# Kernel with adjacency blocks turned by DMA, selection steps shifted toward pass 1, all neighbour coordinates by lookups, arctangent one slot behind its quotients

## The reference

```python
def _L0_xattn_ref(xyz, points, w_center, w_neighbor):        # xyz = ctx, points = x, both weights = fside
    K = 8; NUM_BLOCKS = 4
    sq = jnp.sum(xyz * xyz, axis=1)
    d2 = sq[:, :, None] + sq[:, None, :] - 2.0 * jnp.einsum('bdn,bdm->bnm', xyz, xyz)
    _, idx = jax.lax.top_k(-d2, K)
    for i in range(NUM_BLOCKS):
        shortcut = points
        p = _lrelu(points)                                    # slope 0.01
        g = _group_point(p, idx_t)                            # the 8 neighbours' columns of p
        c = jnp.einsum('oi,bin->bon', w_center[i], p)
        gn = jnp.einsum('oi,bikn->bokn', w_neighbor[i], g)
        points = (c + gn.sum(axis=2)) / (K + 1.0) + shortcut
    return points

def _L1_xattn_ref(x_loc, x, ...):                             # x_loc = ctx, x = the result above
    idx = _knn(x_loc, 30)                                     # the same distances, 30 nearest
    rel = pts[bidx, idx] - pts[:, :, None, :]                 # first three coordinates are used
    xr, yr, zr = (rel[..., 0], rel[..., 1], rel[..., 2])
    rho = sqrt(x2 + y2 + z2); theta = arctan2(zr, sxy); phi = arctan2(yr, xr)
    feat = concatenate([sph, sph - mean(sph)])                # six features
    h = lrelu(_bn(feat @ W1.T, g1, b1)); h = lrelu(_bn(h @ W2.T, g2, b2)); h = lrelu(_bn(h @ W3.T, g3, b3))
    att = softmax(h[..., 0])                                  # over the 30 neighbours
    return x + einsum('bnkc,bnk->bnc', xk, att)               # xk: the neighbours' columns of x
```

## Time and profile before

| | |
|---|---|
| median of 3 runs | 698.96 us (698.92 to 703.58) |
| the profiled execution | 703.56 us |
| its span, first to last instruction | 701.8 us |
| mean granted TensorE clock | 0.995 of 2.4 GHz |
| busy over the span | TensorE 97%, VectorE 85%, GpSimd 56%, ScalarE 49% |
| selection, from its first step to the last index table | 32.2 to 285.4 us |

### The profile page before, as it was taken

One profiled execution on the slowest core, in us unless ns is written; L12 is line 12 of the kernel. 1 busy time (PEld: TensorE's weight loads), 2 busy tenths in 40 slices (PEclk: granted clock), 3 DMA queues, 4 the chain that ended last, 5 costly groups with the idle time before them and its releaser, 6 DMA issues.

```text
span 701.8 us, 13118 instructions
## 1 busy us (share of the span) xinstructions
PE 679.3 (97%) x5364; PEld 573.4 (82%) x5364; DVE 599.0 (85%) x879; ACT 346.1 (49%) x529; POOL 394.1 (56%) x324
## 2 busy tenths in 40 slices
PE   5999999999999999999999999999999999999998
PEld 4799889878888887788888987987988877778887
DVE  4699999999789899876679998776895999788866
ACT  6456547347525327766694354384473434233210
POOL 2268757664877877310039677558669865610143
PEclk9999999999999999999999999999999999999999
DMA  9630300200000022644532721713627763621125
GB/s 350 192 4 2 120 1 2 90 21 11 1 2 0 2 65 87 221 152 165 164 114 91 116 79 63 118 61 91 105 76 221 126 90 90 182 77 47 46 92 164
DMA packets 39483, 64.89 MB, mean 92 GB/s; under 512 B 16000, under 2 KB 16256, under 8 KB 39424
## 3 DMA queue, kind: packets, MB, share of 16 engines
q1 hardware_dynamic: 30288, 44.61, 18.9%
q0 software_dynamic: 8608, 18.40, 13.7%
q10 hardware_dynamic: 528, 1.05, 0.4%
HBM read 47.92 MB, written 14.82 MB: 89 GB/s over the span
## 4 chain that ended last, share of the span: by engine, by line
PE 60%; DVE 16%; POOL 11%; issue 5%; ACT 4%; DMA 2%; another core or an unknown queue 1%; SPq 0%; POOLq 0%; DVEq 0%; ACTq 0%
PE bank L1669 17%; PE bank L1731 4%; PE bank L1579 4%; PE bank L1693 4%; PE bank L1581 4%; PE bank L1580 4%; PE bank L1694 4%; PE bank L1695 4%; POOL more L660 4%; PE bank L1834 3%; PE bank L1793 3%; PE bank L1836 3%; PE bank L1835 3%; POOL p_second L590 3%; POOL pts_l L601 2%
## 5 line engine op out<-in xcount | busy, mean ns | idle before, releaser
L1669 PE MATMUL bank<-nbr,pts_h 128*128 128x512 f32 (+2 forms) x512 | 192.9, 379 | 3.2 <-POOL pts_l L601 1.6
L1669 PE MATMUL bank<-nbr,pts_l 128*128 128x512 f32 (+2 forms) x512 | 190.1, 374 | 0.0
L590 POOL TENSOR_TENSOR p_second<-p_first,p_second 128x512 f32<-128x512 f32 x58 | 76.4, 1320 | 99.4 <-ACT p_second L868 99.3
L1669 PEld LDWEIGHTS bank<-nbr,pts_h 128*128 128x128 f32 x512 | 96.6, 189 | 20.8 <-POOL pts_l L601 3.4
L1669 PEld LDWEIGHTS bank<-nbr,pts_l 128*128 128x128 f32 x512 | 96.7, 189 | 14.9 <-issue 0.2
L882 ACT CAST pts_h<-bank 128x512 fp32r<-128x512 f32 (+2 forms) x64 | 35.1, 554 | 144.5 <-PE bank L1669 136.0
L1693 PE MATMUL bank<-wT,pts_h 128*128 128x512 f32 x256 | 102.7, 401 | 1.4 <-DVE pts_l L1172 0.7
L1695 PE MATMUL bank<-wT,pts_l 128*128 128x512 f32 x256 | 100.4, 392 | 0.0
L1694 PE MATMUL bank<-wT,pts_h 128*128 128x512 f32 x256 | 100.2, 392 | 0.0
L601 POOL TENSOR_TENSOR pts_l<-p_second,pts_h 128x512 fp32r<-128x512 f32 x58 | 79.1, 1370 | 3.5 <-ACT pts_h L874 2.0
L1579 PE MATMUL bank<-pts_h 128*128 128x512 f32 (+3 forms) x192 | 68.9, 359 | 8.6 <-DVE pts_l L1098 8.1
(11 more groups left out here) (228 smaller groups left out, 1518.5 us busy)
## 6 DMA issues: line engine op xcount, KB each, us to landing
p_rows<-p_second SPq DMA_DIRECT2D x32, 256.0 KB, 2.0
more<-a_rows SPq DMA_DIRECT2D x16, 480.0 KB, 4.7
scratch<-a_rows SPq DMA_DIRECT2D x14, 480.0 KB, 5.0
X<-in_ctx SPq DMA_DIRECT2D x12, 512.0 KB, 6.1
out_dram<-X SPq DMA_DIRECT2D x15, 256.0 KB
more<-in_ctx SPq DMA_DIRECT2D x4, 512.0 KB, 5.7
X<-in_x SPq DMA_DIRECT2D x2, 1024.0 KB, 5.5
x_rows<-X SPq DMA_DIRECT2D x8, 256.0 KB
```

The costliest lines, as they stand in the source:

```text
L590: pool.tensor_tensor(p, a, b, ALU.subtract).then_inc(s_p32, 1)
L1669: mm = pe.matmul(bank[u % 3][:, 0:w], p[:, m, t * P:(t + 1) * P], nbr[b][:, m, hf * HALF:hf * HALF + w], start=(m == 0 and part_ == 0), st ...
```

## The change

**Turns by DMA.** `adj_turn(T)` leaves TensorE. SyncE issues a transposing DMA of the 128x1024 bf16 matrix, from `adj` to `landing(T)`: for tiles 0 to 6 the columns of tile 7 in `nbr0`, which are not yet written, for 7 to 15 a part of `scratch`. Even and odd tiles have a semaphore each. `nbr_out` reads `landing(T)` instead of a PSUM bank, and `adjacency(T + 2)` waits for the landing of T. In SyncE's queue the turns stand among the loads of X: T 0 and 1 ahead of the first two, 2 to 5 behind them, 6 to 9 behind the third, 10 to 15 behind the fourth. `nbr_out` of tile 7 waits for that of tile 6. `ADJ_AT` moves three of the four pairs one slot later.

**Selection.** The extra steps of slots 0 and 1 go from 4 and 1 to 2 and 1; slot 15 gets one more, slot 16 four more. Steps end at slot 41 instead of 43, so `G0` is 42 instead of 44. The index tables move to slots 28, 31, 34 and 42 from 30, 33, 36 and 44.

**Lookups for all tiles.** The 30 indirect DMAs, the table in DRAM with its three loads, and the copy from `near_rows` are gone. 32 lookups instead of 30 begin at slot 43 instead of 45. `M0` is 60 instead of 61.

**Arctangent.** ScalarE issues it one slot behind item 10's slot (at 76, where `NET` has an empty entry now), and item 11 and all later ones keep their slots. `T0` is 109 in both.

The diff, cut to its core:

```diff
+        def landing(T):
+            if T < NT - 1:
+                c0 = (NT - 1) * P + T % 2 * P // 2
+                return nbr0_land[:].bitcast(BF16)[:, :, 2 * c0:2 * c0 + P]
+            o = (SC + 1) * N + T % 2 * HALF
+            return scratch[:, o:o + HALF].bitcast(BF16).rearrange("p (m n) -> p m n", m=NT)
...
-            n = STEPS_AT[g % 16] + {0: 4, 1: 1}.get(g, 0)
+            n = STEPS_AT[g % 16] + {0: 2, 1: 1, 15: 1, 16: 4}.get(g, 0)
...
-        ADJ_AT = {3: (8, 9), 6: (10, 11), 9: (12, 13), 14: (14, 15)}
+        ADJ_AT = {4: (8, 9), 7: (10, 11), 10: (12, 13), 14: (14, 15)}
...
-        ROWS_AT = {30: 0, 33: 1, 36: 2, 44: 3}
+        ROWS_AT = {28: 0, 31: 1, 34: 2, 42: 3}
...
-        M0 = G0 + LOOKUPS // 2 + 2
-
-        GATHER_AT = {16: 2, 17: 2, 18: 2, 19: 2, 20: 2, 21: 2, 22: 2, 23: 2, 32: 3, 33: 3, 34: 3, 35: 3, 36: 1, 37: 1}
+        M0 = G0 + TILES + 2
...
-               ((8, 1),), ((9, 0),), ((9, 1),), ((9, 2),), (10,), (11,), (12,), (13,), (14,), (15,), (16,), ((21, 0),),
+               ((8, 1),), ((9, 0),), ((9, 1),), ((9, 2),), (10,), (), (11,), (12,), (13,), (14,), (15,), (16,), ((21, 0),),
...
-        T0 = M0 + len(NET) + GT
+        T0 = 16 * (ITS - 2) + 13
...
+            def adj_turn(T):
+                sp.wait_ge(s_diag, T + 1)
+                if T == NT - 1:
+                    sp.wait_ge(s_sqmm, 2 * NH)
+                if T >= 2:
+                    sp.wait_ge(s_nbr, T - 1)
+                sp.dma_start_transpose(landing(T), adj[:, T % 2, :]).then_inc(s_adjT[T % 2], 16)
+
+            adj_turn(0)
+            adj_turn(1)
             for i, (t0, t1) in enumerate(((0, 4), (4, 8))):
 
                 sp.wait_ge(s_pl1, KT + 4 + 2 * i)
                 sp.dma_start(X[:, 0, t0:t1], x[0].rearrange("(t p) c -> p t c", p=P)[:, t0:t1]).then_inc(s_x[i], 16)
             for i, (t0, t1) in enumerate(((0, 6), (6, 8))):
 
+                for T in (range(6, 10) if i else range(2, 6)):
+                    adj_turn(T)
                 sp.wait_ge(s_p1, AHEAD)
                 sp.wait_ge(s_v, TILES - 2 if i else NT - 1)
                 sp.dma_start(X[:, 1, t0:t1], x[1].rearrange("(t p) c -> p t c", p=P)[:, t0:t1]) \
                     .then_inc(s_x[2 + i], 16)
-            sp.wait_ge(s_adjT, TILES)
+            for T in range(NT + 2, TILES):
+                adj_turn(T)
+            sp.wait_ge(s_nbr, TILES)
...
-                    done = sum(GATHER_AT[q] for q in GATHER_AT if q < g)
-                    for i in range(done, done + GATHER_AT.get(g, 0)):
-                        if i == 0:
-                            pool.wait_ge(s_tabd, 16 * 3)
-                            pool.wait_ge(s_sel, GT)
-                        pool.indirect_dma_start(
-                            out=near_rows[:, i // K1, i % K1, :], out_offset=None, in_=tab_d,
-                            in_offset=bass.IndirectOffsetOnAxis(ap=idx[:, i // K1, i % K1:i % K1 + 1], axis=0)) \
-                            .then_inc(s_rows, 16)
...
             def nbr_out(T):
-                act.wait_ge(s_adjT, T + 1)
+                act.wait_ge(s_adjT[T % 2], 16 * (T // 2 + 1))
+                if T == NT - 1:
+                    act.wait_ge(s_nbr, T)
                 if T == NT:
                     act.wait_ge(s_sel, NT)
                 act.copy(nbr[T // NT][:, :, (T % NT) * P:(T % NT + 1) * P],
-                         bank[6 + T % 2][:].bitcast(BF16).rearrange("p (m n) -> p m n", m=NT)) \
-                    .then_inc(s_nbr, 1)
+                         landing(T)).then_inc(s_nbr, 1)
...
+                if 10 in NET_AT.get(g - 1, ()):
+                    act.wait_ge(s_mlp, MLP["atan"])
+                    act.activation(pair(6), tmp, ACT.Arctan).then_inc(s_act, 1)
                 for m in NET_AT.get(g, ()):
                     if m == 4:
                         act.wait_ge(s_mlp, MLP["sqrt"])
                         act.activation(slots(6, 2), slots(4, 2), ACT.Sqrt).then_inc(s_act, 1)
-                    if m == 10:
-                        act.wait_ge(s_mlp, MLP["atan"])
-                        act.activation(pair(6), tmp, ACT.Arctan).then_inc(s_act, 1)
...
-                    dve.wait_ge(s_rows, 16 * GT * K1)
-                    link(dve.tensor_copy(near[:, :, 0:GT, :], near_rows[:].rearrange("p t k j -> p j t k")))
...
-            def adj_turn(T):
-                pe.wait_ge(s_diag, T + 1)
-                if T >= 2:
-                    pe.wait_ge(s_nbr, T - 1)
-                for m in range(NT):
-                    mm = pe.transpose(bank[6 + T % 2][:].bitcast(BF16)[:, m * P:(m + 1) * P],
-                                      adj[:, T % 2, m * P:(m + 1) * P], ident_b[:])
-                mm.then_inc(s_adjT, 1)
```

More of the change, by code:

```diff
@@ L77, in build @@
         pts_l = sb("pts_l", [P, KT, N], F32R)
+        with nc.sbuf_tensor("nbr0_land", [P, NT, N], F32) as nbr0_land:
+            pass
         nbr0 = sb("nbr0", [P, NT, N], F32R)
@@ L109, in build @@
         prm = sb("prm", [P, 77], F32)
-        near_rows = sb("near_rows", [P, GATHERED_TILES, K1, 3], F32)
         w_eff = sb("w_eff", [P, 6, 3], F32)
@@ L117, in build @@
         p_d = [nc.dram_tensor(f"p_rows{i}", [N, C], F32, kind="Internal").ap() for i in range(B)]
-        tab_d = nc.dram_tensor("table", [N, 3], F32, kind="Internal").ap()
         x_d = nc.dram_tensor("x_rows", [N, C], F32, kind="Internal").ap()
@@ L269, in build @@
         s_diag = sem("adj_diagonal_ready")
-        s_adjT = sem("adj_transposed")
+        s_adjT = [sem(f"adj_transposed{i}") for i in range(2)]
         s_nbr = sem("nbr_ready")
@@ L428, in _ @@
                                  allow_slow_non_contiguous=True).then_inc(s_prm, 16)
-            for j in range(3):
-                sp.dma_start(tab_d[:, j].unsqueeze(1), ctx[0, 2 - j, :].unsqueeze(1),
-                             allow_slow_non_contiguous=True).then_inc(s_tabd, 16)
+            def adj_turn(T):
[7 more added lines that the diff above has]
+            adj_turn(1)
             for i, (t0, t1) in enumerate(((0, 4), (4, 8))):
@@ L463, in _ @@
             for c in range(CHUNKS):
-                for t in range(2 * CH) if c else range(2 * GT, 2 * CH):
-                    u = 2 * CH * c + t - 2 * GT
+                for t in range(2 * CH):
+                    u = 2 * CH * c + t
                     if u == 0:
@@ L1647, in _ @@
             gram(15)
-            adj_turn(6)
             norms(1)
@@ L1727, in lookup @@
                 pe.wait_ge(s_ar, CHUNKS)
-                b = (GT + u // 2) // NT
+                b = u // (2 * NT)
                 for k in range(KH):
@@ L1742, in side @@
             def side(g):
-                if g == 1:
-                    adj_turn(NT - 1)
-                for T in ADJ_AT.get(g - 1, ()):
-                    adj_turn(T)
                 if g in TURN_AT:
```

29 lines of the change are left out of this document (9 added, 20 removed).

## The result

The changed kernel takes 695.39 us (median of 20 executions, 693.38 to 697.79) against 699.7 us (median of 20, 698.56 to 703.58). The ratio is 0.9932, 95% interval 0.9917 to 0.9947: 4.7 us less, 3.7 to 5.8. The forecast was 2.4 us less: the time lies in its range, but the gain is about twice the forecast one. The profiled executions lie further apart, 703.56 and 694.02 us, because that of before was one of its slowest and that of after one of its fastest.

A forecast was written before the change was run, and what follows sets the result against it. VectorE was taken to bound the kernel up to the gate (first lookup), TensorE behind it. Terms -9.3 + 7.8 - 0.9 = -2.4 us on the median 698.96 gave 696.6 us, with 691 to 703 for 8 in 10.

The forecast's parts named there:

- the gate: VectorE's last index table and TensorE's first lookup behind it (286.19 us before); forecast to come 9.3 us earlier, near 277.
- VectorE's idle time before the gate: First selection step to last index table: 8.0 of VectorE's 9.3 us of waits would be used.
- TensorE's wait for `q_low` that I had near slot 19: TensorE's 1.5 us wait at slot 3 shrinks and one of about its size appears at slot 19.
- What fills it: Before the gate: turns credited 1.0 us (adjacency wait); moved selection steps fill 5.4 at slot 16, 0.3 and 1.3 elsewhere.
- The index tables: Last index table moves from slot 44 to 42, putting two `x_update` behind the gate: 1.3 us.
- Behind the gate: TensorE gets two more weight units (5.4 us) and two more lookups (2.4 us), giving back 7.8 us.
- GpSimd's 30 indirect DMAs go too ...: 0: Slots 0 to 44: removal gains 0, as only 0.8 us of VectorE's waiting was for GpSimd, before the first of them.
- The stall at slot 79: TensorE's 0.7 us wait at 427.43, 0.9 with restart; a slot of lead around the arctangent covers it, gaining 0.9 us.
- DMA transposes: Turns by DMA take 2.3 us each, hidden between GpSimd's diagonal and ScalarE's `nbr_out`; cost 0 us.
- Rival B: DMA transposes much slower than copies, delaying tiles 2, 3 and pass 0; at 6 us each +10.8, 707.4 us; chance 0.12.
- Rival A: TensorE decides before the gate too: -6.9 for turns, its waits also count; -8.0, 691.0 us; chance 0.13.
- Rival C: Slot 16 steps delay `q_low` more than they fill, or first lookups run late; half of 5.4 lost, 699.3 us; chance 0.13.

The follow-up runs named there:

- turn: Kernel before with only the sixteen turns moved from TensorE to transposing DMAs; 697.46 us, ratio 0.9959.
- sel: Kernel before with only the new slots of selection, adjacencies and index tables, turns still on TensorE; 700.33 us, ratio 1.0008.
- turn_look: Changed kernel with the old slots of selection, adjacencies and index tables, without the arctangent's move (lookups from slot 45, network from 62); 697.07 us, ratio 0.9975.
- turn_sel: Kernel before with the transposing DMAs and the new selection, adjacency and index table slots; lookups and arctangent as before; 698.98 us, ratio 0.9995.
- no_atan: Changed kernel with the Arctan in item 10's slot, no empty entry in `NET`, network from slot 61; 695.11 us, ratio 0.9928.
- slow_turn: Changed kernel with each transposing DMA issued, waited for and issued again; 717.62 us, ratio 1.0281.
- pe_turns: Changed kernel with the turns back on TensorE; 697.14 us, ratio 0.9979.

## Why the prediction was right, and where it was not

The forecast (696.6 us, no change over 1%) holds, and its frame too: sum up to the gate, then what TensorE has left. The size doesn't: 2.4 us is below the measured interval of 3.7 to 5.8. The first lookup came 11.6 us earlier, not 9.3; the other two terms fit. Point by point:

- **VectorE's idle time before the gate: right.** 8.0 us were to be filled, 7.7 were (9.3 to 1.6). TensorE's wait for `q_low` that I had near slot 19 is not there: the 1.5 us stayed at slot 3 (143.21), and 1.3 for GpSimd came up at slot 16.
- **What fills it: wrong.** "TensorE is not the one that decides" before the gate was false at slot 16. The 5.4 us wait there was for TensorE through ScalarE, so the turns counted there: in turn alone VectorE's `q_low` of slot 16 comes 3.8 us earlier (194.77 to 191.00). I had put 1.0 us on the turns and the rest on the shift; turn gives 3.8 us at slot 32 by itself, sel 1.0. The two compete for one wait. That the idle time filled came out right is luck in part: it is bounded by the wait, whatever fills it.
- **The index tables: missed.** VectorE's gate came 12.8 us earlier, not 9.3. Its groups for them, before and after:

```profile
L1189 DVE TENSOR_SCALAR scratch<-idx 128x128 uint32<-128x128 uint32 x4 | 2.5, 632 | 0.0
L1192 DVE CAST scratch<-scratch 128x128 bf16<-128x128 uint32 x4 | 2.5, 617 | 0.1
L1190 DVE CAST scratch<-scratch 128x128 f32<-128x128 uint32 x4 | 2.0, 502 | 0.1
L1191 DVE TENSOR_SCALAR scratch<-idx 128x128 uint32<-128x128 uint32 x4 | 0.9, 226 | 0.1
```

```profile
L1191 DVE TENSOR_SCALAR scratch<-idx 128x128 uint32<-128x128 uint32 x4 | 1.3, 314 | 0.0
L1192 DVE CAST scratch<-scratch 128x128 f32<-128x128 uint32 x4 | 0.9, 228 | 0.1
L1194 DVE CAST scratch<-scratch 128x128 bf16<-128x128 uint32 x4 | 0.9, 228 | 0.1
L1193 DVE TENSOR_SCALAR scratch<-idx 128x128 uint32<-128x128 uint32 x4 | 0.9, 228 | 0.1
```

  7.9 us became 4.0, as they no longer run beside GpSimd's work (below). That is not the new slots alone: sel, with the new slots and the indirect DMAs, has 7.4, turn_look, with the old slots and no indirect DMAs, 4.6, turn 8.6 and turn_sel 5.1. With 7.7 of idle time, 1.3 for two `x_update`, 3.9 here and 0.2 for an earlier start the sum is 13.1, near the 12.8 read.
- **Behind the gate: right.** From the first lookup to slot 60 TensorE takes 6.3 us more than before, with 1.7 us less lost to the clock: 8.0, against 7.8.
- **"GpSimd's 30 indirect DMAs go too ...: 0": the term that failed.** I asked only whether VectorE had waited for GpSimd. Nobody had waited in the kernel before, because `w_low` was ready, at 266.4, just ahead of slot 40 at 267.35. The shift made GpSimd later (first piece at 256.76 for 254.73) while TensorE became earlier, and that cover was gone. Here the removal is worth 4.7 us by the ratios of turn_sel and no_atan, net of two lookups. The compound change therefore did not lose what its parts lose one by one. That the removal stood in the same change is luck for this forecast: the same working gave 3.9 us less for turn_sel, which gained nothing.
- **The stall at slot 79: right in size (0.8 to 0.9), wrong in cause.** It is gone without the arctangent's move, and 0.6 of it in turn, whose network is the old one. In the kernel before, one network operation at 404.70 took 1.81 us beside GpSimd operations on landed rows, and in turn 1.17. That would be the 0.6, but in sel it took 2.25 and the wait was only 0.4, so what makes up the stall stays open:

```profile
404.70 1.81 DVE L1224 SCALAR_TENSOR_TENSOR bank<-scratch 128x960 f32<-128x960 f32 x1
```

```profile
399.95 1.17 DVE L1249 SCALAR_TENSOR_TENSOR bank<-scratch 128x960 f32<-128x960 f32 x1
```

- **DMA transposes: covered, as forecast.** 3.0 to 3.7 us by themselves (one 4.4) instead of 2.3, and 5.1 to 7.8 for the three issued right behind a load of X. For tiles 2 and 3 I had 86.2 and 88.5 for the landings; ScalarE's `nbr_out` shows them at 84.6 and behind, with adjacency(4) done 3.3 us before VectorE wants it (91.01):

```profile
84.62 2.00 ACT L800 CAST nbr<-nbr_land 128x1024 fp32r<-128x1024 bf16 x2 [2.44 <-DMA nbr_land<-scratch]
86.52 1.15 ACT L808 ACTIVATE scratch<-scores,minus_one 128x1024 bf16<-128x1024 f32 x1
```

  They land 0.9 and 1.9 us behind the second load of X (83.6), one on the heels of the other, where I had stacked 2.3 us twice. Rival B's mechanism is real (slow_turn), at over twice its price, the clock's part included, and with its main place at slot 16. By the Trainium skill, Advanced Engine Details and Errata, X-Bar Transpose (TRN2), a transposing DMA is as fast as a regular one: 3.2 against 2.3 us for the same bytes, not quite. The 10.5 us estimated from VectorE: DVE Perf Modes, The three transpose paths, of the same Trainium skill, is not what a tile costs here.
- **Rival A** (TensorE decides throughout, -8.0) falls with turn and pe_turns, which give 2.9 and 3.3 us for 6.9 us of transposes.
- **Rival C** (the shift doesn't do what it says, 699.3) is not the changed kernel, whose wait at slot 16 is gone. For turn_sel its outcome came true, by a path that it did not name, GpSimd's queue.

## What to carry to other kernels

A wait of engine A for B that has itself just been waiting for C belongs to C: follow it before you call C's time free. Two edits that fill the same wait don't add, and what an instruction off the path costs is asked again once the path or its queue has moved. List for each queue what becomes ready less than the expected gain ahead of its use, and what else the edit puts ahead of it. Then try moving the one or two instructions that hold it before removing the whole feature.
